# Gate rows sent per batch, preparations reordered around chunk 0, and the small operations of two norms done together

## The reference

```python
mod = (silu(c) @ wmod).reshape(8, 6, 1, -1)
sa, ca, ga, sb, cb, gb = (mod[:, i] for i in range(6))
ga = (2 * (ga >= 0) - 1) * maximum(abs(ga), 0.25)      # gb likewise
h = layernorm(x) * (1 + ca) + sa
x = x + ga * linear_attention(h)       # 16 heads of 16, rotary, elu + 1, causal
h = layernorm(x) * (1 + cb) + sb
x = x + gb * mixture(h)                # 8 experts of width 1024, top 2, gelu
```

## Time and profile before

| What | us |
|---|---|
| median of 3 runs (942.12 to 943.51) | 942.8 |
| the profiled execution's own time | 944.19 |
| its span | 942.5 |
| busy: PE, DVE, ACT, POOL | 749.9, 702.9, 600.1, 522.5 |

### The profile page before, as it was taken

How to read it: one execution, slowest core, us unless ns; L and a number is a source line. 1 busy time by engine, 2 the same in 40 slices (tenths; PEclk the granted TensorE clock), 3 DMA queues, 4 the chain that set the end, 5 groups by cost and what they waited for, 6 DMA issues and landing times.

```text
span 942.5 us, 27031 instructions
## 1 busy us (share of the span) xinstructions
PE 749.9 (80%) x8190; PEld 555.1 (59%) x8191; DVE 702.9 (75%) x1579; ACT 600.1 (64%) x1167; POOL 522.5 (55%) x521
## 2 busy tenths in 40 slices
PE   3327777777788787887416699999999999999995
PEld 0115555555555565555315477777777777777773
DVE  4138888888888888887489377777777777777773
ACT  2137878787787878886200376667666767667763
POOL 3125777777767777775229344445444544454532
PEclk9557989899988989997559799999999999999998
DMA  4441223232323222221000233333333333333320
GB/s 159 155 113 52 92 80 101 75 106 78 106 78 106 78 74 89 79 87 45 29 0 0 67 75 71 67 67 71 70 72 67 67 74 71 68 66 68 77 39 1
DMA packets 49884, 69.24 MB, mean 73 GB/s; under 512 B 6080, under 2 KB 40144, under 8 KB 49832
## 3 DMA queue, kind: packets, MB, share of 16 engines
q0 software_dynamic: 15904, 27.02, 14.5%
q1 hardware_dynamic: 33928, 41.54, 14.0%
HBM read 51.71 MB, written 21.94 MB: 78 GB/s over the span
## 4 chain that ended last, share of the span: by engine, by line
PE 46%; POOL 20%; issue 20%; DVE 6%; ACT 4%; SPq 1%; DMA 1%; POOLq 1%; ACTq 0%; DVEq 0%; PEldq 0%
PE hidden L1251 13%; PE bank L1267 13%; POOL h L779 9%; PE hidden L1253 7%; PE bank L1269 6%; POOL x L793 3%; POOL kst L787 3%; POOL rstd L771 2%; ACT h L878 2%; POOL xt L816 2%; PE bank L1104 2%; SPq L1285 1%; PE hidden L1104 1%; DVE amlo L480 1%; PE bank L1021 1%
## 5 line engine op out<-in xcount | busy, mean ns | idle before, releaser
L1251 PE MATMUL hidden<-qstT,w1hi_k 128*128 128x256 f16 x1136 | 200.9, 274 | 0.0
L1253 PE MATMUL hidden<-qstT,w1lo_k 128*128 128x128 f16 x1136 | 196.2, 220 | 0.0
L1267 PE MATMUL bank<-w,amhi 128*128 x568 | 188.5, 379 | 5.1 <-issue 4.6
L1269 PE MATMUL bank<-w,amlo 128*128 x568 | 154.8, 273 | 0.0
L850 POOL DMA_INDIRECT out_dram<-x,si x71 | 113.0, 1592 | 44.9 <-DVE x L711 22.5
L731 DVE TENSOR_TENSOR amlo<-am,amhi 128x512 f16<-128x512 f32 x142 | 98.3, 692 | 50.9 <-ACT am L1009 50.9
L779 POOL TENSOR_TENSOR h<-h,am 128x256 f32<-128x256 f32 x128 | 105.7, 825 | 27.0 <-ACT h L878 20.6
L1251 PEld LDWEIGHTS hidden<-qstT,w1hi_k 128*128 x1136 | 111.8, 98 | 13.8 <-issue 0.2
L771 POOL TENSOR_TENSOR rstd<-var,minus_half 128x1 f32<-128x1 f32 x64 | 46.4, 725 | 125.3 <-DVE var L425 125.3
L1253 PEld LDWEIGHTS hidden<-qstT,w1lo_k 128*128 x1136 | 111.7, 98 | 1.6 <-issue 0.2
L1267 PEld LDWEIGHTS bank<-w,amhi 128*128 128x128 f16 x568 | 55.6, 98 | 66.3 <-issue 6.8
(11 more groups left out here) (202 smaller groups left out, 2039.0 us busy)
## 6 DMA issues: line engine op xcount, KB each, us to landing
stage<-in_L_ffn_w_dram SPq DMA_DIRECT2D x32, 512.0 KB, 3.7
xt<-in_L_attn_x_dram SPq DMA_DIRECT2D x32, 128.0 KB, 3.4
am<-mod_rows SPq DMA_DIRECT2D x16, 256.0 KB, 3.8
ffn_rows<-mod_rows SPq DMA_DIRECT2D x1, 4096.0 KB
out_dram<-x SPq DMA_DIRECT2D x32, 128.0 KB, 1.7
ffn_rows<-h SPq DMA_DIRECT2D x32, 128.0 KB, 1.7
w<-in_L_wmod_dram SPq DMA_DIRECT2D x6, 256.0 KB, 3.7
out_dram<-x,si POOLq DMA_INDIRECT x71
```

Source lines behind the costliest of these rows:

```text
L1251: t.matmul(dst.rearrange("p (q n) -> p q n", q=2), w1s[0][k][g][:, w_], both, start=(k == 0), stop=False)
L1253: last = t.matmul(dst[:, P:2 * P], w1s[1][k][g][:, w_], both[:, 0, :], start=False, stop=(k == KT - 1))
L1267: t.matmul(y[:, :], ghi[:, m.p, c_m], w2s[mt // 2][:, bass.ds(w_, 2 * D)], start=(mt == 0), stop=False)
L1269: last = t.matmul(y[:, D:2 * D], glo[:, m.p, c_m], w2s[mt // 2][:, bass.ds(w_, D)], start=False, stop=(mt == MT - 1))
```

## The change

The transfer of the second gate becomes eight transfers of one batch (512 KB) each, issued from a new last entry `("gb", 3)` of `ORDER_SP` when the chunk three steps back is the second of its batch. At the start only the first two modulation rows (shift and scale of the first norm) are computed ahead of chunk 0. The conditioning row is transposed first and its silu done on 128 partitions. ACT, no longer SP, issues the write and the load of these two rows. The split of the attention weights moves behind `hhi` (ACT) and `hlo` (DVE) of chunk 0, and PE waits for it ahead of `v` of chunk 0. The other four modulation rows are computed on PE after step 0 and on DVE after step 1; SP sends them after its step 1. Four chunks of x and two pieces are loaded ahead of the pipeline, not two and one. In each step one `ve`, one `rs` and one `nb` serve both norms, on two columns. The five orders change: `pj` stands ahead of `hT`, `stl` right behind `ve`, `sl1` ahead of `hlo`, `sh1` ahead of `xn2`, `kTs` ahead of `h2Te`, `pv1` ahead of `v`, and on SP `ld` has lag 2 and stands behind `ldx`, with `ro` ahead of `so`.

```diff
-ORDER_PE = (("aT", 4), ("ear", 3), ("sc1", 3), ("hT", 0), ("pj", 4), ("pv0", 3), ("h2T", 6), ("Tk", 2), ("v", 0),
-            ("state", 2), ("Tq", 2), ("pv1", 3), ("lg", 6), ("sc0", 2), ("qk", 0))
+ORDER_PE = (("aT", 4), ("ear", 3), ("sc1", 3), ("pj", 4), ("hT", 0), ("h2T", 6), ("pv0", 3), ("Tk", 2), ("pv1", 3),
+            ("v", 0), ("state", 2), ("Tq", 2), ("lg", 6), ("sc0", 2), ("qk", 0))
+ORDER_DVE = (("st", 0), ("st2", 5), ("mv", 0), ("mv2", 5), ("ve", 0), ("stl", 3), ("f", 2), ("nb", 0), ("sl0", 3),
+             ("alo", 4), ("rope", 1), ("t1", 4), ("sl1", 3), ("hlo", 0), ("wlo", 2), ("den", 3), ("rec", 3),
+             ("vlo", 0), ("at", 3))
+ORDER_POOL = (("rs", 0), ("xm", 0), ("h", 0), ("slo", 2), ("R", 1), ("xm2", 5), ("x1", 4), ("h2", 5))
+ORDER_ACT = (("exp", 2), ("sh0", 3), ("xn", 0), ("ahi", 4), ("shi", 2), ("sh1", 3), ("xn2", 5), ("hhi", 0),
+             ("whi", 1), ("kTs", 2), ("h2Te", 6), ("vhi", 0), ("sth", 2), ("qTs", 2), ("lge", 6))
-ORDER_SP = (("ldx", 0), ("so", 5), ("ro", 6), ("ld", 1), ("moda", 1), ("modg", 5), ("modb", 6))
+ORDER_SP = (("ldx", 0), ("ld", 2), ("ro", 6), ("so", 5), ("moda", 1), ("modg", 5), ("modb", 6), ("gb", 3))
...
+            def steadied(m):
+
+                wait(dve, a_["mv"], m.n + 1, NC)
+                wait(dve, a_["mv2"], m.n - NORM2 + 1)
+                wait(dve, a_["rs"], m.n)
+                v.tensor_scalar(var[:, :], mv[:, :, 1], LN_EPS, None, ALU.add).then_inc(a_["ve"], 1)
...
+            def gate_rows(m):
+
+                if m.c == 1:
+                    b = bass.ds(m.b, 1)
+                    carry(sp)
+                    sp.dma_start(rows_d.rearrange("(b s) n -> b s n", b=B)[b, :, D:2 * D],
+                                 mod_d[b, MOD["gb"]:MOD["gb"] + D].rearrange("b (u d) -> b u d", u=1)
+                                 .broadcast_to([1, S, D])).then_inc(s_gb, 16)
...
+            def rest_of_modulation():
+
+                pe.wait_ge(s_ld["rw"], 16)
+                for k in range(KT):
+                    t.transpose(bank[7][:, k * E:(k + 1) * E], rw_raw[:, k * P:(k + 1) * P], ident[0:E, 0:E])
+                pe.wait_ge(s_ld["wmod"], 16 * KT * 2)
+                modulation_of(1)
+                modulation_of(2).then_inc(s_pe, 1)
...
+                if isinstance(m.n, int) and m.n == 0:
+                    weights_of_attention()
```

More of the change, by code:

```diff
@@ L58 @@
 Q_SCALE = float(HD ** -0.25)
-ORDER_PE = (("aT", 4), ("ear", 3), ("sc1", 3), ("hT", 0), ("pj", 4), ("pv0", 3), ("h2T", 6), ("Tk", 2), ("v", 0),
-            ("state", 2), ("Tq", 2), ("pv1", 3), ("lg", 6), ("sc0", 2), ("qk", 0))
[L62 to L67, removed]
-ORDER_SP = (("ldx", 0), ("so", 5), ("ro", 6), ("ld", 1), ("moda", 1), ("modg", 5), ("modb", 6))
+ORDER_PE = (("aT", 4), ("ear", 3), ("sc1", 3), ("pj", 4), ("hT", 0), ("h2T", 6), ("pv0", 3), ("Tk", 2), ("pv1", 3),
[7 more added lines that the diff above has]
+ORDER_SP = (("ldx", 0), ("ld", 2), ("ro", 6), ("so", 5), ("moda", 1), ("modg", 5), ("modb", 6), ("gb", 3))
+NORM2 = 5
+BOTH_NORMS = ("ve", "rs", "nb")
 LAG_C = 2
@@ L242, in adaln_block @@
                             " state sth stl ear sc0 sh0 sl0 sc1 sh1 sl1 pv0 pv1 den rec at aT ahi alo pj"
-                            " t1 x1 st2 mv2 ve2 rs2 nb2 xn2 xm2 h2 h2T h2Te lg lge whi wlo")
+                            " t1 x1 st2 mv2 xn2 xm2 h2 h2T h2Te lg lge whi wlo")
         s_x = [sem(f"s_x{c}") for c in range(CPB)]
@@ L251, in adaln_block @@
         s_row = [sem("s_row0"), sem("s_row1")]
-        s_ld = {k: sem("s_ld_" + k) for k in ("c", "wmod", "wq", "wo", "rw", "cos", "sin")}
+        s_ld = {k: sem("s_ld_" + k) for k in ("c", "wmod0", "wmod", "wq", "wo", "rw", "cos", "sin")}
         s_pool = sem("s_pool")
@@ L283, in step, with steps_a @@
                     m = a.back(lag)
-                    if m.inside(NC):
+                    if m.inside(NC + NORM2 if name in BOTH_NORMS else NC):
                         works[name](m)
             return step
-        def steps_a(eng, step, order, after_first=None):
+        def steps_a(eng, step, order, after=None, when=0):
             for c in range(2 * CPB):
                 step(At(0, c, CPB))
-                if c == 0 and after_first:
-                    after_first()
+                if c == when and after:
+                    after()
             with eng.Fori(2, B - 1) as b:
@@ L384, in modulation @@
-            def modulation(rows):
-                for k, add in rows:
-                    o = MOD[k]
[L388 to L409, removed]
@@ L410, in _, with weights_of_attention @@
-            dve.wait_ge(s_pool, POOL_CONST)
+            dve.wait_ge(s_pe, PE_MOD_A)
+            for k, add in (("sa", 0.0), ("ca", 1.0)):
+                o = MOD[k]
+                link(v.tensor_scalar(mod_s[0][:, o:o + D], bank[MOD_BANK[0]][0:B, o:o + D], add, None, ALU.add))
+            marks["mod_a"] = link.n
+            dve.wait_ge(s_pool, POOL_CONST)
+            def weights_of_attention():
+                dve.wait_ge(s_act, ACT_W)
+                for raw, hi, lo in ((wq_raw[0], wqhi[:, 0, :], wqlo[:, 0, :]),
+                                    (wq_raw[1], wqhi[:, 1, :], wqlo[:, 1, :]),
+                                    (wo_raw, wohi[:, :, :], wolo[:, :, :])):
+                    link(v.scalar_tensor_tensor(out=lo, in0=raw, scalar=WS, in1=hi, op0=ALU.mult, op1=ALU.subtract))
+                marks["wo"] = link.n
@@ new lines, in rest_of_modulation @@
+            def rest_of_modulation():
+                dve.wait_ge(s_pe, PE_MOD)
+                rows = hidden[1][0:B, :, :].rearrange("p i n -> p (i n)").rearrange("p (q n) -> p q n", n=D)
+                rw_ps = bank[7][:, 0:KT * E].rearrange("p (k e) -> p k e", k=KT)
+                link(v.tensor_copy(rw32[:, :, :], rw_ps))
+                gates = rows[:, 0:4:3, :]
+                link(v.tensor_scalar(gate_s, gates, 0.0, 1e30, ALU.is_ge, ALU.mult))
+                link(v.scalar_tensor_tensor(out=gate_a, in0=gate_s, scalar=-GATE_MIN, in1=gates,
+                                            op0=ALU.add, op1=ALU.min))
+                link(v.tensor_scalar(gate_s, gates, 0.0, -1e30, ALU.is_lt, ALU.mult))
+                for q, k in enumerate(("ga", "gb")):
+                    o = MOD[k]
+                    link(v.scalar_tensor_tensor(out=mod_s[o // (4 * D)][:, o % (4 * D):o % (4 * D) + D],
+                                                in0=gate_s[:, q, :], scalar=GATE_MIN, in1=gate_a[:, q, :],
+                                                op0=ALU.add, op1=ALU.max))
+                for q, (k, add) in enumerate((("sb", 0.0), ("cb", 1.0))):
+                    o = MOD[k]
+                    link(v.tensor_scalar(mod_s[o // (4 * D)][:, o % (4 * D):o % (4 * D) + D], rows[:, 1 + q, :],
+                                         add, None, ALU.add))
+                marks["mod"] = link.n
@@ L419, in mean_var, with offset @@
                 v.bn_aggr(mv[:, k, :], st[:, k, :]).then_inc(a_[done], 1)
[L421 to L432, removed]
+            def steadied(m):
[3 more added lines that the diff above has]
+                v.tensor_scalar(var[:, :], mv[:, :, 1], LN_EPS, None, ALU.add).then_inc(a_["ve"], 1)
+            def offset(m):
+                wait(dve, a_["rs"], m.n + 1)
+                wait(dve, a_["xn"], m.n, NC)
+                wait(dve, a_["xn2"], m.n - NORM2)
+                v.scalar_tensor_tensor(out=nb[:, :], in0=mv[:, :, 0], scalar=-1.0, in1=rstd[:, :],
+                                       op0=ALU.mult, op1=ALU.mult).then_inc(a_["nb"], 1)
             def first_stats(m):
@@ L436, in first_stats @@
                 stats(x_slot(m), 0, "st")
[L438 to L443, removed]
             def h_rest(m):
@@ L459, in rope @@
                 wait(dve, a_["qk"], m.n + 1)
+                if isinstance(m.n, int) and m.n == 0:
+                    dve.wait_ge(s_ld["cos"], 16)
+                    dve.wait_ge(s_ld["sin"], 16)
                 wait(dve, a_["exp"], m.n)
@@ L765, in _, with root @@
             link(g.tensor_copy(rev[:, :], iota_i[:, 0:E]))
[L767 to L771, removed]
+            def root(m):
+                wait(pool, a_["ve"], m.n + 1)
+                wait(pool, a_["nb"], m.n)
+                wait(pool, a_["xn"], m.n, NC)
+                wait(pool, a_["xn2"], m.n - NORM2)
+                g.tensor_tensor(rstd[:, :], var[:, :], minus_half[:, :], ALU.pow).then_inc(a_["rs"], 1)
             def modulated(m, dst, rows, part, op, ready, loaded, done):
@@ L863, in copy, with weights_of_attention @@
                 return v.activation(out_, in_, ACT.Copy, scale=scale)
[L865 to L871, removed]
-            act.wait_ge(s_pool, POOL_CONST)
+            act.wait_ge(s_pe, PE_C)
+            v.activation(c_exp, bank[0][:, 0:KT * B].rearrange("p (k b) -> p k b", k=KT), ACT.Exp, scale=-1.0)\
+                .then_inc(s_act, 1)
+            act.wait_ge(s_dve, marks["mod_a"])
```

(31 more changed lines are left out.)

93 lines of the change are left out of this document (48 added, 45 removed).

## The result

The changed kernel takes 953.8 us (4 runs, 952.46 to 954.55) against 942.5 before, a ratio of 1.012 (95% interval 1.010 to 1.013). It is slower; 909 had been predicted. Its profiled span is 952.2 us, 9.7 more than before.

What follows compares the result with a forecast made beforehand. No engine was full; a chain through several set the 12.19 us step. Start 16 plus 29 steps at 0.6 (17.4) gave 33.4 off the profiled 944.19, less 1.4 to the median: 909 us, range 893 to 931.

Steps and rivals of the forecast that it cites:

- The large transfer: Second gate's DRAM-to-DRAM transfer on SP's queue: one batch, 512 KB, on all 16 engines at 362 GB/s, 1.45 us.
- Rival D: Each one-batch gate transfer runs on one engine, stalling seven batches about 20 us each: 1050 us, chance 0.03.
- The rest of the sum: Start 16 us and 29 steps 17.4 us, together 33.4 us saved; emptying of the pipeline and later stages 0.
- The piece arrives later: Piece issued later on SP, so ACT waits for it: charged 1.6 us per batch, 0.4 a step.
- The charge for `gb`: Extra lateness of the piece when the gate transfer stands ahead of it on SP: 0.7 + 1.45 = 2.2 us.
- The start: Up to chunk 2: DVE's 21.9 us wait for x goes, `nb` starts at 41.7 to 45.0, gain 16 us.
- The two norms together: Each step loses a `ve` and a `nb` on DVE, gaining 0.3 us, and one power on POOL, taken as 0.
- The orders: In each step `pj` no longer waits for `hT`; with the norms' 0.3, a step is 1.0 us shorter.
- ACT's 1.12 us: ACT's wait for `nb` before `xn`, taken as 1.12 us a step and as the limit on a step's shortening.

Runs made afterwards that it cites:

- e3: Changed kernel with each of the eight gate transfers taking 64 rows of every batch (eight source rows), not 512 rows of one: 921.3 us.
- e12: e3 with the 64 rows outermost and the eight batches inside in each gate transfer: 916.0 us.
- e5: Changed kernel with one entry of SP's order moved, gb right behind ld, ahead of ro and so: 912.0 us.
- e4: Changed kernel with the 512 rows of each gate transfer written as 8 times 64, all from one source row: 962.8 us.
- e6: e1 with the SP order of the kernel before, ld with lag 1 right behind ro: 904.2 us.
- e1: Changed kernel with the old single 4 MB gate transfer, issued behind SP's last step, in place of the eight: 914.3 us.
- e8: e7 plus the new orders of PE, DVE, POOL and ACT; start and SP's order as before the change: 899.2 us.
- e2: Kernel before, with only its 4 MB gate transfer moved behind SP's last step: 920.7 us.
- e10: e8 with the two norms apart as before (a power, a ve and an nb each): 892.8 us.
- e7: e2 with the two norms done together; orders and start as before the change: 932.6 us.

## Why the prediction was wrong

- **The large transfer: the step that failed.** "I take 1.45 us, since the loads with 128 rows outermost are the nearest rows." It took over 7, at 70 GB/s. The row was the wrong neighbour: those loads read 128 different rows of DRAM, this transfer reads one row 512 times. The old transfer read eight, and its half rate was put down to the number of engines. That was right: with 64 outermost the share goes from 0.57 to 0.90 and the rate from 166 to 299 GB/s (e3, e12). But the changed transfer had more than half of the engines at work (0.79) and still moved 65 GB/s. The text weighed the shape against the Trainium skill ("DMA: Bandwidth & Descriptors", on why a DMA increments its semaphore by 16) and asked nothing about the source; that rule says how many engines take part, not how fast one row can be read. The traces agree with it: 0.57 with 8 outermost, 0.90 with 64, and up to 0.79 in the changed transfer.
- **Rival D was right in kind.** Its point of decision was a stall of more than 4.8 us per gate transfer; e5 puts it at 41.8 / 7 = 6.0, for six long steps and one stall in the emptying. Its mechanism, one engine, isn't what the runs show: more than half of the engines were at work (0.79), and the same shape as the old one, with one source row, is slow as well (e4). It had 0.03.
- **The rest of the sum came out near, in part by luck.** With the gate transfer behind the piece and all else as changed, the kernel takes 912.0 (e5), 3 us above 909. Terms that were wrong cancel there: a loss by the joint norms where a gain was priced, and a faster PE that wasn't priced at all (below).
- **The piece arrives later: right, size of one term wrong.** The charge for `gb` was 0.7 + 1.45 us; it should have been 0.7 + 7. With the gate gone the later piece costs 0.2 to 0.4 us a step (e6 against e1); the charge was 0.4 with the gate in it, so that it fits is in part luck.
- **The start: right in sum, wrong in what it was held against.** `nb` of chunk 2 started at 42.38, which lies in 41.7 to 45.0, in place of 59.18: 16.8 us won. `v` of chunk 0 came late, at 25.14 and not 23.2, as the write of the first rows took from 9.24 to 14.10, not 1.5 us, while the loads kept the DMA engines busy (386 GB/s from 9 to 14 us), and `xm` started at 17.45, not 15.3. But all of the gain is the stop taken away; next to the old start without it the reordering lost 4 us up to chunk 2 (e6 against e8).
- **The two norms together: wrong in sign.** Priced at -0.3 us a step on DVE and 0 on POOL; measured +0.1 to +0.4. Under the old orders DVE had time to spare (busy for 85% of a stretch of 303 us in e2), and the chain through the two-column power got longer by 0.15 us. What costs under the new orders stays open.
- **The orders: about right in size, the reason in part.** The forecast was 1.0 us a step with 0.3 from the norms in it, so some 0.7 for the orders. Measured it is 0.84 with the norms apart (e2 and e10, 12.12 to 11.28) and 1.14 with them joint (e7 and e8). The shorter wait before `t1` was seen, but ACT's 1.12 us was per wait, and over all steps of that stretch it is 0.97; the clock, 0.92 in e2 and 0.99 in e10 over the stretch above, was not.

## What to carry to other kernels

Ask of a transfer in a queue not only how many bytes it moves but how many different places it reads, and put what is needed soon ahead of it: one entry moved was worth 42 us here. Before crediting a reordering with the end of a stall, take the stall away alone; the rest of the change may be a loss, as the new start and the joint norms were. A group of small operations on a chain isn't cheaper for being fewer, when the engine had time to spare.

## What the runs showed of the hardware

Copies from DRAM to DRAM that read one 1 KB row over and over moved 65 to 73 GB/s with 512 rows outermost, at a DMA share of 0.40 to 0.79, and 58 with 8 outermost. With eight source rows it was 166 to 179 GB/s with 8 outermost and about 300 with 64. The runs with eight source rows also wrote to eight places. And a reordering of PE that adds no work and takes none away moved the granted clock in the steps from 0.93 to 0.99.
